# Row and column scores of three attentions on one ring of three pairs of PSUM banks

## The reference

```python
# attention 0: causal, relative bias      attention 1: causal, product of two scores
att = q @ k.T / sqrt(D) + bias            logits = (q1 @ k1.T) * (q2 @ k2.T) * SCALE
att = where(causal, -inf, att)            logits = where(causal, -inf, logits)
# attention 3: no mask
scores = q @ k.T / sqrt(HD)
# all three
out = softmax(scores) @ v;  x = x + out @ wo.T + bo
```

## Time and profile before

| | us |
|---|---|
| median of 3 runs | 1576.62 (1574.43 to 1581.41) |
| the profiled execution | 1574.67 |
| its span | 1573.0 |
| attention 0, fill, both passes, drain | 134 to 362 |
| attention 1 | 590 to 835 |
| attention 3 | 1207 to 1447 |

### The profile page before, as it was taken

The page is one execution under the profiler, slowest core; times in us unless marked ns, Lnnn a source line. Parts: engine busy times, 40 slices in busy tenths (PEclk is TensorE's granted clock), DMA queues, the critical chain, the costliest instruction groups (busy, mean ns, idle before and its releaser), DMA issues. The chain is left out here.

```text
span 1573.0 us, 27316 instructions
## 1 busy us (share of the span) xinstructions
PE 1274.5 (81%) x10265; PEld 707.7 (45%) x10273; DVE 865.6 (55%) x2261; ACT 633.6 (40%) x1318; POOL 490.1 (31%) x552
## 2 busy tenths in 40 slices
PE   3995889886978758999997976682995899899498
PEld 2662333333664535556553642432673223333277
DVE  4056567632145457667634557794137888782305
ACT  1321455451313135665552224241334577665043
POOL 5653012112320067667200001125563022121442
PEclk9996899887979979999997978695996699997699
DMA  6622422102720036655506300002342221210244
GB/s 129 159 76 81 106 73 73 39 9 67 226 61 11 1 114 199 174 169 153 162 27 83 53 7 1 0 14 84 101 127 80 66 69 35 73 32 11 80 120 122
DMA packets 147502, 128.46 MB, mean 82 GB/s; under 512 B 19102, under 2 KB 133162, under 8 KB 147377
## 3 DMA queue, kind: packets, MB, share of 16 engines
q1 hardware_dynamic: 138432, 114.08, 26.8%
q0 software_dynamic: 6304, 11.37, 2.2%
q10 hardware_dynamic: 2640, 1.36, 0.6%
HBM read 79.80 MB, written 47.69 MB: 81 GB/s over the span
## 5 line engine op out<-in xcount | busy, mean ns | idle before, releaser
L2463 DVE TENSOR_REDUCE att_maxima<-psum 128x2 f32<-128x1024 f32 (+3 forms) x384 | 355.0, 950 | 162.0 <-PE psum L2108 71.6
L2344 ACT ACTIVATE att_probs<-psum 128x512 f32<-128x512 f32 (+1 forms) x640 | 320.8, 554 | 263.4 <-PE psum L2142 94.2
L108 POOL TENSOR_TENSOR rstd<-var_eps,neg_half 128x4 f32<-128x4 f32 x44 | 45.0, 1024 | 549.2 <-DVE var_eps L99 548.9
L2123 PE MATMUL psum<-att_queries,att_keys 50*128 50x512 bf16 (+3 forms) x512 | 131.9, 370 | 29.2 <-ACT att_probs L2344 17.0
L1045 POOL DMA_INDIRECT returned<-moe_out,moe_slot_tokens x101 | 101.4, 1004 | 117.8 <-DVE moe_out L973 90.8
L839 ACT ACTIVATE moe_hidden<-psum,moe_b 128x320 f32<-128x320 f32 (+1 forms) x128 | 77.7, 607 | 125.8 <-PE psum L752 123.9
L172 PE MATMUL psum<-ident,normalised_rows 128*128 128x128 f32 x192 | 44.0, 372 | 96.2 <-DVE normalised_rows L117 73.5
L759 PE MATMUL psum<-moe_w,moe_hidden 128*128 128x128 f32 (+1 forms) x784 | 109.5, 286 | 0.0
L2084 PE MATMUL psum<-att_keys,att_queries 48*128 48x512 bf16 (+3 forms) x512 | 94.2, 384 | 17.4 <-DVE att_maxima L2463 15.6
L2181 PE MATMUL psum<-att_probs,att_values 128*32 128x512 f32 (+3 forms) x1024 | 98.8, 461 | 0.8 <-ACT att_context_t L2351 0.8
L752 PE MATMUL psum<-moe_slot_columns,moe_w 128*128 128x320 f32 (+1 forms) x256 | 96.5, 520 | 2.9 <-ACT moe_slot_columns L834 2.9
(11 more groups left out here) (297 smaller groups left out, 2269.2 us busy)
## 6 DMA issues: line engine op xcount, KB each, us to landing
score_terms<-att_parts SPq DMA_DIRECT2D x44, 384.0 KB, 3.0
moe_w<-l_w SPq DMA_DIRECT2D x64, 256.0 KB
moe_back<-returned SPq DMA_DIRECT2D x24, 256.0 KB, 4.5
att_queries<-score_terms SPq DMA_DIRECT2D x64, 96.0 KB
att_keys<-score_terms SPq DMA_DIRECT2D x64, 96.0 KB
att_queries<-score_terms SPq DMA_DIRECT2D x16, 384.0 KB, 4.3
att_keys<-score_terms SPq DMA_DIRECT2D x16, 384.0 KB, 5.3
dispatched<-untaken SPq DMA_DIRECT2D x2, 2064.0 KB, 25.9
```

The lines of the kernel that those rows point to most:

```text
L2123: mm = nc.tensor.matmul(dst, k_op[half, i, p, key], q_op[half, i, p, query], start=c0 == 0, stop=kind == 3, skip_group_check=True)
L2344: nc.scalar.activation(probs[:, G % 2, 2 * p + r, unit_at[u]:unit_at[u] + w], g.psum[:, cols_bank + r, 0:w], ACT.Exp).then_inc(probs_ready, 1)
L2463: ins = nc.vector.tensor_reduce(maxima[:, G % 2, t, 2 * p:2 * p + 2], g.psum[:, rows_bank(k):rows_bank(k) + 2, c0:c0 + w], axis=AX, op=ALU ...
```

## The change

Rows and columns share one ring of three pairs of banks (0 and 1, 2 and 3, 4 and 5). A unit takes the next pair in the order in which TensorE makes them: rows k of group n+2 has place 2(k - 2X), columns k of group n has place 2k + 1, and the pair is the place modulo three. So each unit must wait for the reader of the unit three places before: rows for both exponentials of the columns two steps before (in the fill, for the maximum of rows k-3), columns for the maximum of the rows of the step before (in the drain, for the exponential of the columns three steps before). Nothing else in the program changes; the counts waited for are these:

```diff
-        rows_bank = lambda k: 2 * (k % 2)
-        cols_bank = 4
+        rows_bank = lambda k: 2 * (2 * (k - 2 * X) % 3)
+        cols_bank = lambda k: 2 * ((2 * k + 1) % 3)
+        lag, last = 2 * X, NG * X
...
             def rows_unit(G, p, u):
                 i, k = G % RING, G * X + p * U + u
-                if k >= 2:
-                    pe.wait_ge(rows_taken, k - 1)
+                if k - lag >= 2:
+                    pe.wait_ge(probs_ready, 2 * (k - lag - 1))
+                elif k >= 3:
+                    pe.wait_ge(rows_taken, k - 2)
...
             def columns_unit(G, p, u, r):
-                i, k, j = G % RING, 2 * (G * X + p * U + u) + r, 2 * p + r
-                if k >= 2:
-                    pe.wait_ge(probs_ready, k - 1)
+                i, k, j = G % RING, G * X + p * U + u, 2 * p + r
+                if k - 1 + lag < last:
+                    pe.wait_ge(rows_taken, k + lag)
+                else:
+                    pe.wait_ge(probs_ready, 2 * (k - 3) + r + 1)
                 c0 = 0
                 for s in units[u]:
-                    dst = g.psum[:, cols_bank + r, c0:c0 + width[s]]
+                    dst = g.psum[:, cols_bank(k) + r, c0:c0 + width[s]]
...
-                                         g.psum[:, cols_bank + r, 0:w], ACT.Exp).then_inc(probs_ready, 1)
+                                         g.psum[:, cols_bank(G * X + x) + r, 0:w], ACT.Exp).then_inc(probs_ready, 1)
```

More of the change, by code:

```diff
@@ L2134, in columns_bias @@
             def columns_bias(G, p, u):
-                c0, pair = 0, PAIRS * (G % GROUPS) + p
+                k, c0, pair = G * X + p * U + u, 0, PAIRS * (G % GROUPS) + p
                 for s in units[u]:
@@ L2141, in columns_bias @@
                             half = slice(HALF * r, HALF * (r + 1))
-                            mm = nc.tensor.matmul(g.psum[strip, cols_bank + r, c0:c0 + w], flips[half, :],
+                            mm = nc.tensor.matmul(g.psum[strip, cols_bank(k) + r, c0:c0 + w], flips[half, :],
                                                   bias_kq[half, pair, STRIP * c:STRIP * c + w], start=False, stop=True,
@@ L2147, in columns_bias, with columns_mask @@
                     c0 += width[s]
-            def columns_mask(r, u):
-                c0 = 0
+            def columns_mask(G, p, r, u):
+                k, c0 = G * X + p * U + u, 0
                 for s in units[u]:
-                    mm = nc.tensor.matmul(g.psum[:, cols_bank + r, c0:c0 + P], g.identb[:], g.mask_kq[:],
+                    mm = nc.tensor.matmul(g.psum[:, cols_bank(k) + r, c0:c0 + P], g.identb[:], g.mask_kq[:],
                                           start=False, stop=True, skip_group_check=True)
@@ L2326, in _ @@
                         for r in range(2):
-                            columns_mask(r, u)
+                            columns_mask(n, p, r, u)
                     if x in turn_at:
```

## The result

| kernel | median us | runs |
|---|---|---|
| before | 1579.33 | 11 |
| changed | 1589.01 (1583.41 to 1596.62) | 11 |

The ratio is 1.0077, 95% interval 1.0054 to 1.0099: about 12 us slower. The forecast was 1587.5, a loss of 10.9 us. The profiled execution of the changed kernel took 1583.41 us, its span is 1581.7 at a mean granted clock of 0.885.

The account below looks back on a forecast made before the run. TensorE is full in attention 1, near-full with VectorE in attention 3. Attentions 1, 0 and 3 sum 10.7 - 1.4 + 1.6 = +10.9 us on 1574.67: 1585.6 beside it, 1587.5 as median, range 1574 to 1600.

Parts of the forecast that it names:

- The waits of attention 1: Attention 1, columns of steps 1 and 4: they wait for VectorE's maximum, 0.50 and 0.58 us more, +12.3 us in all.
- The hand-over: From the end of VectorE's reduction to TensorE's released work: 0.07 us taken, bounds 0.07 to 0.20.
- Attention 3's slot: Attention 3, plain slots: 0.4 to 0.5 us longer each from 12.67, taken as 0.35 x 13 = +4.6 us.
- Attention 0's step: Attention 0: one wait replaces the other, 1.99 us per step against 1.93, taken as +1.5 us over 14 slots.
- VectorE's late work: Attention 0, ahead of step 0's reduction: value copies and row normalisations now reach TensorE, 4.3 us, half taken, 2.1.
- D: Rival, much slower: attention 3 pays 0.8 us each slot, three to five slots lose their clock at 2.8: 1600 us, chance 0.08.
- The drains: Ends of the attentions, TensorE's idle for exponentials goes: -4.0 us in attention 0, -1.6 in attention 1, -1.0 in attention 3.
- the fills: Starts of attentions 0 and 3: VectorE's idles of 0.99 us behind projections go, -1.0 and -2.0 us.
- B: Rival, faster: columns of steps 1 and 4 lose the wait on exponentials and gain none, about 1560 us, chance 0.10.
- C: Rival, no change: fills, drains, fetch stalls and attention 0 give back attention 1's 10.7 us, about 1578 us, chance 0.27.
- The rows' new wait: Rows wait for exponentials of two steps before: seldom last, a pair taking 1.09 us with a whole step of 1.93 more.

Follow-up runs that it names:

- the ends alone: Kernel before with old banks and waits in steady slots, third pair lent to rows in fills, rows' pairs to columns in drains: 1557.3 us, ratio 0.9877.
- the drains without the fills: Kernel before with only the drain's columns using all three pairs, fill and steady slots as before: 1536.44 us beside 1556.29, ratio 0.9876.
- halved maxima: Reduction over the first half of the columns only: kernel before so cut 1533.44 us (0.9861), changed kernel so cut 1502.92 (0.9658), beside 1556.29.

## Why the prediction held, step by step

**The waits of attention 1: right, with a term a little small.** Forecast 1.60 us from mask to columns, measured 1.59; 1.29 from the start of the reduction at step 1, measured 1.28; about 1.1 us more a slot, measured 15.23 (663.93 to 679.16) against 14.17 (668.45 to 682.62). The hand-over is 0.06 in both rows above, the near end of its bounds. The sum was +12.3, the steady slots lost 15.3. The missing 3 us are mostly places: 28 waits for maxima were counted where I had 23, 13 of them of 0.77 us where I had priced 10, 15.4 us where "near 12" was written. By the windows of the steady slots TensorE's idle grew from 7.4 to 20.4 us, the 15.4 less what had been waits for exponentials; the other 2.3 us are busy time, for the same number of matmuls. The earlier trace rows hold only the columns of attentions 0 and 3; attention 1's waits for exponentials, 4.1 us, stand in a row of their own.

**Attention 3's slot: right.** The earlier trace rows gave 12.67 us; after, two transposes a slot apart give it:

```profile
1269.47 0.66 PE L2197 MATMUL psum<-ident,att_context_t 128*128 128x128 f32 x4
1272.34 0.39 PE L2128 MATMUL psum<-att_queries,att_keys 50*128 50x512 bf16 x2 [0.22 <-DVE att_maxima L2468]
1282.46 0.66 PE L2197 MATMUL psum<-ident,att_context_t 128*128 128x128 f32 x4
```

12.99 us, 0.32 more, where 0.35 was the mean taken and 13.15 the figure for a slot of this kind. Steady +6.2 against +4.6 in the sum, at the same clock of 0.91. Here too the two waits trade places: the idle for maxima is 22.4 us, but the columns are busy for 47.1 us where they were for 66.3, a saving that the forecast followed only through the reductions and never priced.

**Attention 0's step: right in size.** The earlier trace rows gave 1.93 between two row biases, the forecast 1.99:

```profile
209.02 0.30 PE L2107 MATMUL psum<-bias_qk,flips 64*32 64x256 f16 x8
209.40 1.23 DVE L2468 TENSOR_REDUCE att_maxima<-psum 128x2 f32<-128x1024 f32 x1 [1.56 <-PE psum L2107]
210.68 0.40 PE L2128 MATMUL psum<-att_queries,att_keys 50*128 50x384 bf16 x4 [0.92 <-DVE att_maxima L2468]
211.00 0.36 PE L2107 MATMUL psum<-bias_qk,flips 64*32 64x256 f16 x16
```

1.98. The bracket has grown from 0.39 to 0.92 and the step by 0.05 only, since the columns now take 0.40 in place of 0.88. With the ring in attention 0 alone the steady slots took 6.2 us more than before, at 0.92 against 0.93, where the sum had 3.6.

**VectorE's late work: the mechanism right, one place under-priced.** I took 2.1 us in all. One stall alone took 2.89, where a norm (L117, 1.48 us from 239.30) and the maxima's splitting stood ahead of step 0's reduction:

```profile
240.90 1.07 DVE L2485 TENSOR_TENSOR att_max_parts<-att_maxima,att_max_parts 128x16 bf16<-128x16 f32 x1
242.00 0.31 DVE L2489 STREAM_TRANSPOSE att_max_t<-att_max_parts 128x128 bf16<-128x128 bf16 x1
242.24 1.19 DVE L2468 TENSOR_REDUCE att_maxima<-psum 128x2 f32<-128x1024 f32 x1
243.48 0.40 PE L2128 MATMUL psum<-att_queries,att_keys 50*128 50x384 bf16 x4 [2.89 <-DVE att_maxima L2468]
```

The first row is slow by itself: the like operation two slots later (268.43) took 0.18 us. Of the 48 such operations in each kernel 15 and 13 took 0.48 us or more, and beside every one of them GpSimd ran an operation for about as long (here from 240.78 to 241.93); a few of the short ones had it beside them too, so this is a likely cause and not a shown one. The kernel before has the same 1.07 us at 239.86, and TensorE does not wait for it there. The clock fell behind the stall, by the windows:

```profile
242.00:244.00 2.00, 0.52 (x14) 0.27 (x21) 1.42 (x2) 0.00 (x0) 1.76 (x2) 0.96 0.35 113
244.00:246.00 2.00, 2.00 (x40) 1.19 (x28) 1.29 (x2) 1.29 (x3) 0.00 (x0) 0.50 0.09 25
```

That is D's mechanism, in attention 0 and not in 3. But this stall is not all of it. The longest stretches at clock 0.50 in attention 0's steady slots, from 291.6 to 301.8 and from 308.7 to 318.9 us, follow no such stall: in the 10 us before either of them TensorE's waits were of 0.97 us at most. Why the clock fell there stays open. In attention 1, whose waits are 0.2 to 0.8 us each, the clock stayed at 1.00. The Trainium skill (TensorE: Matmul & The Clock Gate, "A second HAM failure mode: psum-queue depth-cycling") ties the swing of the clock to short idles from cycling through PSUM banks; by the trace 28 such idles in attention 1 did not bring it about, and in attention 0 the trace leaves room for it.

**The drains: the term that was mis-sized.** The sum had -4.0, -1.6 and -1.0, and -3.0 for the fills: -9.6. The forecast's bound let them give 2 us more (and its other end, nothing given, would be +9.6 and not +8); the ends alone measured -19.4, the drains without the fills as much in ratio. Hence the steady slots cost about 12.2 + 19.4 = 31.6 us, if the two parts add, where the sum had 12.3 + 3.6 + 4.6 = 20.5. The traces of before and changed give 12.3 + 15.3 + 6.2 = 33.8, a lower clock in attention 0 included; with attention 0 taken from the kernel that has the ring there alone it is 27.7. Both sides were 7 to 11 us small, and the errors cancelled. That the time came within 2 us of the forecast is partly luck; that the kernel is slower, and that the wait in attention 1 makes it so, is not. What made the drains small is the way I priced them, by the idle time of the array. By the drains' windows above, idle fell by 3.3 us in attention 0 and 0.5 in attention 3, where I had taken 4.0 and 1.0, but busy time fell by 4.3 and 6.0 us, which I had put at nothing. The earlier trace rows show the 4.7 us of idle, but not that 10.2 us at clock 0.50 (337.8 to 348.0) begin inside that stall. Kernel before:

```profile
338.37 1.08 ACT L2344 ACTIVATE att_probs<-psum 128x512 f32<-128x512 f32 x2 [3.36 <-DMA x_rows<-x]
339.02 0.88 PE L2123 MATMUL psum<-att_queries,att_keys 50*128 50x256 bf16 x2 [2.71 <-ACT att_probs L2344]
```

nor the 0.88 us that such columns take; in the changed kernel a group like it took 0.28 (344.16). There the clock was full, so this difference holds both the late second head and the clock. In attention 3's drain only 1.8 us of idle for exponentials was shown, yet 6.5 us went. Attention 1's, at full clock, gave 2.6 against 1.6. How much of the 7 us each in attentions 0 and 3 is wait and how much clock is settled only roughly. The drains of attention 3 with the old banks took 29.2, 25.8 and (halved maxima) 23.1 us at clocks of 0.77, 0.94 and 1.00, with the new ones 22.7, 21.7 and 19.1 to 20.2 at 0.85, 0.92 and 1.00. At like clock that leaves 3 to 4 us for the waits, the hidden ones included. In attention 0 the old banks took 26.1 to 27.2 us at 0.80 to 0.81, the new ones 21.2 to 21.9 at 0.84: 4 to 6 us, a little of it clock.

**The rivals.** B is out: att_maxima releases the columns. C had the direction of what the drains do, but its give-back had to meet a loss of 28 to 32 us, not 20. The rows' new wait does not bite: in the changed kernel TensorE's array never idles before L2087 for an exponential; the waits that end with one are the weight loads', ahead of a busy array.

## What to carry to other kernels

Before you share a ring of banks between two kinds of results, see that the slower reader is done in time, or issue its input first: the same ring was +0.8% with the mask behind the columns and -1.7% with it ahead, where that order alone gave -0.4%. The old banks with deeper drains and the mask ahead reached the same -1.7%, so the ring as such bought nothing there that shows. Where one of the two streams has ended, lend its banks to the other: that alone gave 1.2%, and in attention 1, where it can be read, it cost nothing in the steady slots (195.7 both times). And price a wait by the length of the matmul groups as well as by the idle before them: a group of two or four that starts in pieces is counted as busy.

## What was not expected of the hardware

Two products of 50 rows each, for two heads in the two halves of the array, take 0.38 us when they start together and 0.83 when the second is held back. The wait that staggers them costs more than its idle time shows: the columns of attentions 0 and 3 were busy for 40.6 us less when it was gone. A stall of TensorE of 2.9 us (240.59 to 243.48) was followed by 2 us at clock 0.50, while waits of 0.2 to 0.8 us, one or two a slot, left it at 0.99 to 1.00 for the whole of attention 1. And a VectorE operation that mostly takes 0.18 us took 1.07 while GpSimd ran one beside it.
